# Gates of a mixture-of-experts kernel moved from GpSimd to VectorE, expert numbers loaded ahead of attention's last product, and all engines' orders set anew

## The reference

```python
x = x + attention(_layernorm(x), ctx_768, Wq, bq, Wk, bk, Wv, bv)     # one head, width 256
x = x + ffn(_layernorm(x), Wr, W1, b1, W2, b2)

def ffn(x, Wr, W1, b1, W2, b2):                                       # E = 8, M = 1024, K = 2
    probs = softmax(einsum('bsh,eh->bse', x, Wr))
    top_v, top_i = top_k(probs, 2);  top_v = top_v / sum(top_v)
    for e in range(8):
        w_e = sum(where(top_i == e, top_v, 0))
        h = gelu(einsum('bsh,mh->bsm', x, W1[e]) + b1[e])
        out += (einsum('bsm,hm->bsh', h, W2[e]) + b2[e]) * w_e
```

## Time and profile before

| what | us |
| --- | --- |
| median of 3 runs | 364.0 (363.49 to 366.4) |
| the profiled execution's own time | 360.23 |
| its span, first to last instruction | 358.5 |
| PE busy | 328.6 (92% of the span) |
| ACT busy | 241.6 (67%) |
| DVE busy | 226.2 (63%) |
| POOL busy | 217.0 (61%) |
| mean granted TensorE clock | 0.979 |

### The profile page before, as it was taken

The page is one execution under the profiler, slowest core; times in us unless marked ns, Lnnn a source line. Parts: engine busy times, 40 slices in busy tenths (PEclk is TensorE's granted clock), DMA queues, the critical chain, the costliest instruction groups (busy, mean ns, idle before and its releaser), DMA issues.

```text
span 358.5 us, 10330 instructions
## 1 busy us (share of the span) xinstructions
PE 328.6 (92%) x3428; PEld 284.6 (79%) x3428; DVE 226.2 (63%) x520; ACT 241.6 (67%) x493; POOL 217.0 (61%) x248
## 2 busy tenths in 40 slices
PE   8879999989899769999999999999999999999930
PEld 8637758846666559889999999999999999999920
DVE  3156779889789988687755555554654555555520
ACT  1559889999796647567666666767667766766610
POOL 5525915016866657787866676674665676676731
PEclk9999999999999989999999999999999999999985
DMA  7995576736912148444374444344534442522221
GB/s 250 356 342 187 194 272 174 285 119 205 324 46 74 59 129 171 99 63 141 70 82 62 61 64 52 55 53 55 62 44 48 63 57 35 64 31 33 31 29 15
DMA packets 51602, 40.85 MB, mean 114 GB/s; under 512 B 29248, under 2 KB 47296, under 8 KB 51424
## 3 DMA queue, kind: packets, MB, share of 16 engines
q1 hardware_dynamic: 41024, 26.97, 27.7%
q0 software_dynamic: 7584, 10.57, 17.5%
q10 hardware_dynamic: 2944, 2.66, 2.2%
HBM read 22.40 MB, written 12.66 MB: 98 GB/s over the span
## 4 chain that ended last, share of the span: by engine, by line
DMA 44%; PE 23%; DVE 12%; issue 10%; POOL 4%; ACT 3%; POOLq 1%; SPq 1%; DVEq 0%; ACTq 0%
DMA out<-y,meta 39%; PE o_ps L657 4%; DMA x_sb<-x 4%; PE s_ps L638 3%; PE o_ps L791 3%; PE proj L604 2%; PE s_ps L774 2%; PE proj L625 2%; PE t_ps L774 2%; POOL rows L479 2%; DVE w2h L1097 2%; PE proj L612 1%; ACT w2h L866 1%; PE t_ps L648 1%; DVE negmax L1134 1%
## 5 line engine op out<-in xcount | busy, mean ns | idle before, releaser
L515 POOL DMA_INDIRECT out<-y,meta x39 | 67.3, 1727 | 57.0 <-DMA out<-y,meta 34.5
L1035 ACT ACTIVATE g<-s_ps,b_sb,down 128x128 f32<-128x128 f32 x156 | 62.9, 453 | 41.5 <-PE s_ps L774 40.5
L1464 DVE TENSOR_SCALAR gh<-g,up 128x512 f16<-128x512 f32 x78 | 39.9, 512 | 76.9 <-ACT g L1035 76.5
L791 PE MATMUL o_ps<-w2h,gh 128*128 x312 | 85.1, 273 | 0.4 <-DVE gl L1466 0.4
L791 PE MATMUL o_ps<-w2h,gl 128*128 x312 | 85.0, 273 | 0.0
L791 PE MATMUL o_ps<-w2l,gh 128*128 x312 | 85.0, 273 | 0.0
L1035 ACT ACTIVATE g<-t_ps,b_sb,down 128x128 f32<-128x128 f32 x156 | 62.6, 452 | 24.5 <-PE t_ps L774 20.6
L774 PE MATMUL s_ps<-xs,w1h 128*128 128x128 f16 x624 | 60.4, 220 | 3.0 <-issue 3.0
L774 PE MATMUL t_ps<-xs,w1h 128*128 128x128 f16 x624 | 61.3, 221 | 0.0
L1466 DVE SCALAR_TENSOR_TENSOR gl<-g,up,gh 128x512 f16<-128x512 f32 x78 | 58.8, 753 | 2.8
L774 PEld LDWEIGHTS s_ps<-xs,w1h 128*128 x624 | 47.9, 98 | 6.5 <-issue 3.1
(11 more groups left out here) (191 smaller groups left out, 547.1 us busy)
## 6 DMA issues: line engine op xcount, KB each, us to landing
staged<-W1T SPq DMA_DIRECT2D x6, 1024.0 KB, 6.8
staged<-W2T SPq DMA_DIRECT2D x3, 1024.0 KB, 10.6
w1h<-W2T SPq DMA_DIRECT2D x3, 1024.0 KB, 5.5
x_sb<-x SPq DMA_DIRECT2D x4, 512.0 KB, 4.0
w1l<-W1T SPq DMA_DIRECT2D x2, 1024.0 KB, 12.0
w2l<-W2T SPq DMA_DIRECT2D x2, 1024.0 KB, 11.1
out<-x_sb ACTq DMA_DIRECT2D x4, 512.0 KB, 3.0
rows<-send POOLq DMA_DIRECT2D x8, 130.0 KB, 6.7
```

The source lines that it names most:

```text
L515: pool.indirect_dma_start(out=out, out_offset=bass.IndirectOffsetOnAxis(ap=meta[:, t % META, 3:4].bitcast(I32), axis=0), in_=y2[:, t % YR, ...
L791: i = nc.tensor.matmul(y_ps[t % 2][:, 0:D], l[:, t % 2, m, :], second_weight(w, m, e), start=(m == 0 and k == 0), stop=(m == MC - 1 and k ...
L1035: i = nc.scalar.activation(g[:, t % 2, m, :], h_ps[s][:, (m % MQ) * TR:(m % MQ + 1) * TR], ACT.Gelu, bias=b1_sb[:, bass.ds(e, 1), m:m + 1] ...
L1464: nc.vector.tensor_scalar(gh[:, u, m, :], g[:, u, m, :], by, None, ALU.mult).then_inc(g_high, 1)
```

## The change

Five things are edited.

1. `mark(t)` goes from POOL to DVE. It is still three instructions. DVE issues `mark(0)` behind `split(0, 0)` and `mark(t + 1)` behind `split(t + 1, 0)`.
2. PE waits for the tables and loads the experts' numbers of tiles 0 and 1 between `attend(3, 2)` and `attend(3, 3)`, attention's last product.
3. On POOL, `send_rows(0, 1)` comes ahead of `split_low(1)` and of the root for batch 3's first norm, and all of batch 2's and 3's sends come behind `scatter(0)`.
4. On ACT, DVE and SP the order in the attention stage changes in many places; `LOW_ORDER` and `HIGH_ON_SCALAR`, which count the units in that order, follow.
5. At tile 2, PE computes batch 3's logits straight behind its turned rows, and the ranks at tile 3; ACT takes them at the tile's start, and DVE's `route_gates(3)` moves from tile 2 to tile 3, beside `late_tables_2`.

```diff
-LOW_ORDER = (0, 1, 2, 5, 3, 4, 6, 7, 9, 8, 11, 10, 13, 12, 14, 15)
+LOW_ORDER = (0, 1, 3, 2, 5, 4, 6, 9, 8, 7, 10, 11, 13, 12, 14, 15)
...
             send_rows(0, 0)
+            send_rows(0, 1)
+            split_low(1)
             tokens(1)
-            split_low(1)
             rsqrt(0, 3, ln_var, ln_rstd)
-            send_rows(0, 1)
             rsqrt(1, 2, ln2_var, ln2_rstd)
             send_rows(1, 0)
             send_rows(1, 1)
             split_low(2)
+            rsqrt(1, 3, ln2_var, ln2_rstd)
+            split_low(3)
+            tokens(2)
+            tokens(3)
...
             for t in range(TILES):
                 if t == EARLY:
                     pool.wait_ge(stored, 16 * B)
-                if t + 2 < TILES:
-                    mark(t + 2)
+                scatter(t)
                 if t == 0:
+                    send_rows(2, 0)
+                    second_exps(3)
                     send_rows(2, 1)
                 if t == 1:
-                    tokens(3)
-                if t == 2:
+                    send_rows(3, 0)
                     send_rows(3, 1)
-                scatter(t)
-                if t == 0:
-                    second_exps(3)
-                if t == 1:
-                    send_rows(3, 0)
...
                 if not last:
                     turn_x(b + 1)
+                else:
+                    pe.wait_ge(tables_ready, 1)
+                    e_of = {0: expert(0), 1: expert(1)}
                 attend(b, 3)
...
                 if (t, m) == (2, 2):
                     turn_normal(B - 1)
-                if (t, m) == (2, 3):
+                if (t, m) == (2, 2):
                     logits(B - 1)
-                if (t, m) == (2, 7):
+                if (t, m) == (3, 0):
                     ranks(B - 1)
...
+                if t == 2:
+                    store(2)
+                    turned_rows("x2t", 3)
+                    rows_hi(3)
...
             soft(3, 0)
             turned_rows("x2t", 2)
+            take_logits(2)
             soft(3, 1)
+            take_turned(3, 0)
+            take_turned(3, 1)
+            second_exps(2)
+            soft(3, 2)
+            rows_hi(2)
             high(14)
-            take_turned(3, 0)
-            soft(3, 2)
-            take_logits(2)
-            rows_hi(2)
-            take_turned(3, 1)
             take_turned(3, 2)
             soft(3, 3)
+            take_turned(3, 3)
             high(15)
-            take_turned(3, 3)
-            second_exps(2)
...
+            def mark(t):
+
+                v = t % YR
+                if t == 0:
+
+                    dve.wait_ge(o_full, NT)
+                dve.wait_ge(meta_in[t % META], meta_landed(t))
+                first, second, choice = (meta[:, t % META, k:k + 1] for k in range(3))
+                now = fresh[:, t:t + 1]
+                if t >= YR:
+
+                    dve.wait_ge(y_ready, t - YR + 1)
+                nc.vector.tensor_scalar(gates[:, v, 0:1], choice, rank_of[:, t:t + 1], now, ALU.is_equal,
+                                        ALU.mult).then_inc(marked, 1)
+                dve.wait_ge(marked, t * 3 + 1)
+                nc.vector.scalar_tensor_tensor(out=gates[:, v, 1:2], in0=first, scalar=second, in1=gates[:, v, 0:1],
+                                               op0=ALU.subtract, op1=ALU.mult).then_inc(marked, 1)
+                dve.wait_ge(marked, t * 3 + 2)
+                nc.vector.scalar_tensor_tensor(out=gates[:, v, 2:3], in0=second, scalar=now, in1=gates[:, v, 1:2],
+                                               op0=ALU.mult, op1=ALU.add).then_inc(marked, 1)
...
                 if t + 1 < TILES:
                     split(t + 1, 0, e_of[t + 1])
+                    mark(t + 1)
...
-                if t == 2:
+                if t == 3:
                     route_gates(3)
-                if t == 3:
                     late_tables_2()
```

149 lines of the change are left out of this document (60 added, 89 removed).

## The result

The changed kernel takes **364.6 us** (median of 12 runs), the kernel before 362.6 on the same chip (12 runs): ratio 1.0061, 95% interval 1.0032 to 1.0091, some 2.0 us slower. I had forecast 0.7 us faster. The time lies in my range and in the "within 1%" band, but the sign is wrong, by more than the measurement's uncertainty.

A forecast was written before the change was run, and what follows sets the result against it. The line of scatters was taken to set the end, at the third scatter plus 36 x 4.96 us. A third scatter 0.7 us earlier gave 359.5 from the profiled 360.2, or 363.3 against the median; 8-in-10 range 359 to 367.5.

The forecast's parts named there:

- "within 1%" band: Whole kernel: a time from 360.4 to 367.6 us, given a chance of 0.58.
- the gain of 0.7 at POOL's seam: POOL where the experts begin: first scatter at 145.1, third at 171.2 instead of 171.88, so 0.7 us gained.
- The rule for the end: Experts' stage: the end is the third scatter's start plus 36 x 4.96 us, if later than PE allows.
- `mark` on DVE, zero per step: Experts' tiles: removing marks from POOL saves 0 per tile, since they ran during the scatter's DMA flight.
- rival C: Experts' scatters: DVE's extra work lengthens each step; at 0.12 us a step, 367.6 us in all; chance 0.08.
- the 1.2 I had added: PE at tiles 1 and 3, where DVE also makes tables: 0.6 us of stall each, bounds 0 and 2.4.
- The loads, -1.5: PE ahead of attention's last product: early loads start the experts' stage at 129.4, gain 1.5 us, bounds 0 and 2.7.
- Attention, 0 with bounds -2.5 to +4.5: Attention stage: closed norm waits and the eight sends ahead of batch 3's root sum to 0 us.
- Rival B: POOL in attention: eight sends make batch 3's root late, 98.9 for 94.42; +3.8 us, 367.8 in all; chance 0.12.
- The clock: PE from 130 to 150 us: one idle gap fewer takes back 0.7 us of slow clock, bounds 0 and 1.8.

The follow-up runs named there:

- after_again: The changed kernel, unedited, measured once more: ratio 1.0071 to the kernel before, which takes 363.7 us on that chip.
- e10_all: The changed kernel with the old orders of POOL, ACT and DVE through attention; orders from the experts' start on stay new: ratio 1.0084 to the kernel before.
- e5_both: The kernel before with marks on DVE and the experts' numbers loaded ahead of attention's last product, all old orders kept: ratio 0.9936.
- e7_pool: The changed kernel with only POOL's order through attention set back: ratio 0.9993 to the kernel before.
- g2_both: The kernel of e5_both, unedited, measured again on a chip of the slower kind: ratio 1.0100 to the kernel before.
- f1: The kernel of e9 repeated on another chip of the slower kind: ratio 1.0221 to the kernel before.
- f2: Repeat of e5_both plus only the new orders of PE, ACT, DVE and SP from the experts' start, slower kind of chip: ratio 1.0202 to the kernel before.
- e12: e5_both with sends spread round the first scatters and tile 0's first split earlier on DVE, slower kind of chip: ratio 0.9990 to the kernel before.
- g1: e12 with batch 3's eight sends all behind the second scatter, slower kind of chip: ratio 1.0086 to the kernel before.
- e9: e5_both plus only POOL's new order from the third split on, slower kind of chip: ratio 1.0221 to the kernel before.

## Why the prediction was wrong, by its own steps

The forecast put the third scatter at 171.2; in `after_again` it came at 174.16, 3.0 us later, by these steps:

| step | forecast | after_again | e10_all |
|---|---|---|---|
| stage start | 129.4 | 130.91 | 129.39 |
| to the end of tile 0's weighing | 15.5 | 16.42 | 16.72 |
| to the first scatter | 0.2 | 0.92 | 0.93 |
| to the third scatter | 26.1 | 25.91 | 26.41 |

**The step that failed is the gain of 0.7 at POOL's seam**: it needed the loads' 1.5 us to reach the first scatter whole, and it set the new order against the old one with its marks still in. `e10_all` has the stage start that I forecast and its third scatter is still 2.25 us late. The runs put the cost of all the new orders from the experts' start on at 1.5% (0.9936 without, 1.0084 with them), where I had a gain.

**The rule for the end** (third scatter plus 36 steps) held for the changed kernel on kind A: in `after_again` the third scatter is 2.28 us later than before, the step 4.956 us for 4.959, the last scatter 2.17 us later; the medians are 2.0 apart in the first comparison, 1.6 on this chip. It doesn't hold in `e5_both`, where PE sets the end, nor on kind B.

**`mark` on DVE, zero per step: not contradicted.** Steps in line-bound profiles were 4.93, 4.96, 5.02 and 5.04 us with the marks on DVE (the last in the slower execution of `e7_pool`), 4.96 in the one without. They scatter by 0.1 us, which over 36 steps is 3.8 us, nearly what rival C needed, so a longer step can't be told from none. What rival C started from points the other way: with 17 us more work on DVE from 190 to 340 the scatters took 1.65 us on POOL on average in the result's profile, for 1.73 before. DVE still waits 1.12 us for gelu ahead of a split, and PE's stalls where DVE also makes tables are 1.09 us at 157.17 and 0.77 at 178.51 in the result's profile (the second has no releaser there; in `after_again` the like one, 0.81 us, is put down to the tables), 1.9 for the 1.2 I had added (bound 2.4). What I did not see is that the marks also paced the sends.

**The loads, -1.5: right at the stage's start, not behind it.** In `e10_all`, with attention's old orders, the stage started where I said. That is partly luck: `e5_both` has the same orders there but for one load, and starts at 131.51, since it was 2.8 us behind by 82 us already. But I had followed the gain only to PE's first product, not to tile 0's end. There `e10_all` is 0.2 us later than before, and `e5_both`, measured from attention's last product, 1.0 us earlier. The cover I failed to name was DVE's queue, whose rows for 128 to 131 (2.90 us busy of 3.00) I had quoted.

**Attention, 0 with bounds -2.5 to +4.5: late, but not shown to cost.** `after_again` starts the stage 1.5 us later than `e10_all`, which has the old orders there, but 0.6 us earlier than `e5_both`, which has them too. Rival B's mechanism did happen: in `after_again` the root ended at 97.43 (B had 98.9, before 94.42), and the turned rows came at 98.90, 2.9 us later than before (B: 4.5 later). Most of it reached the stage's start: `after_again` starts the stage where the kernel before does (130.91), although the idle of 2.97 us at the loads and the wait of 2.08 us for ACT ahead of attention's last product are gone there. The last scatter is 2.2 us later than before, where B had 3.8. But the medians of `e10_all` and `after_again` (365.9 and 365.3) show no gain from the old orders.

**The clock:** from 130 to 150 it was 0.91 in `after_again`, as before, and 1.00 in the result's profile and in `e10_all`, so the 0.7 that I took back was there in some executions and not in others. It fell elsewhere too: in `after_again` PEclk is 0.50 from 85 to 90, behind the wait of 1.73 us for batch 1's logits, and 0.91 from 60 to 100, where before it is 1.00; in the result's profile it is 0.66 from 100 to 105, behind the 2.95 us ahead of the turned rows.

**POOL's seam, -0.7: the sum from first to third was right, the conclusion not.** I had 26.1 us; they were 26.4 and 25.9. But I forecast the first scatter at 145.1, and in `after_again` it came at 148.25, 3.1 later: 1.5 from the stage's start, 0.9 from there to the end of tile 0's weighing, where PE waited 1.33 us for DVE (I had nothing), and 0.7 because the scatter started 0.92 us behind the weighing and not 0.2. The new order hangs the third scatter on tile 0 with nothing done in advance, so each microsecond there goes to the third scatter. In the old order the first scatter waits for POOL's own sends, 5.2 us behind the weighing in `e5_both` (147.77 to 152.99), and from the stage's start to the third scatter it takes 38.9 us, against 44.1. I had weighed the new seam against the old one with its marks in, never against the old one without them.

**What stays open.** On kind A, G was seen in the profiles of `e5_both` and `e10_all` but not isolated, because its runs fell on kind B; which of the new orders at the seam costs how much is not shown. PE's line relative to the stage's start was near the same in both (tile 36 weighed after 210.0 and 210.4), which speaks for G and against F. What sets the length of a step is open too. On kind B the reason for PE's and ACT's halts is unknown. The queues that bring instructions have the same share of DMA time in all profiles (0.5 to 0.6% and 0.1 to 0.2%), so nothing is seen there of slower transfers of instructions. There POOL's new order seems to add another 1% to `g2_both`, and the other engines' new orders too (f1 1.0221, f2 1.0202, for 1.0100); the interval of f2 overlaps that of g2, and neither is explained. The kernel before was not profiled on kind B.

**A better version:** on kind A `e5_both` beats both kernels (361.5 against 363.7 and 365.3). On kind B it does not (1.010), and e12 is level with the kernel before; e12 on kind A was not measured.

## What to carry to other kernels

Follow a gain past the instruction that it moves, to the next one that needs another engine: a stall of PE closed by an early load came back in part 5.6 us later, as a wait of 1.76 us for VectorE. When work is taken out of a queue, ask what it had kept apart and what could now be done in advance there; compare a new order with the old one minus that work. And measure more than once, on more than one chip, before an order is called better: the two operations with the old orders are 0.6% faster on one kind and 1.0% slower on the other.

## What the runs showed of the hardware

Six measurements of the kernel before, on at least five chips, fell into two kinds: 362.6 and 363.7 us, and 367.8 to 370.0. In the second kind TensorE stops with no releaser for up to 1.7 us at a time near the indirect row scatters between the first tiles: 5.0 to 9.9 us in sum from 134 to 190 where eight of them (128 rows each) are issued 1.27 us apart, 3.0 to 4.2 where at most four are. One edit separates 3.0 from 6.9 (e12, g1, on two chips of the kind). Why is open, and the eight in a row of attention have no such idle in most kernels. Where the holes were dense, the clock was lower as well: 0.72 from 160 to 190 in e9, where PE was busy 22.0 of 30 us (PE, PEld, DVE, ACT, POOL, then PEclk, as in the earlier trace rows):
```profile
160.00:190.00 30.00, 22.03 (x205) 17.19 (x205) 13.72 (x35) 11.16 (x29) 14.64 (x13) 0.72 0.29 77
```
Loads of registers on TensorE's queue are hidden where products are queued ahead of them: in the changed kernel the 16 matmuls at 129.81 follow each other in 3.62 us with both experts' numbers loaded in between, against 2.97 us of idle when the loads stood alone, in front of the stage.

Three dependent instructions of VectorE on one number per partition (a mark) took 0.27, 0.22 and 0.22 us, 0.78 us from the first's start to the last's end (`e10_all`, 134.77 to 135.55).
